# A state-space scan loop in units of two states, with softplus summed by TensorE

## The reference, cut to what matters

```python
dt = jax.nn.softplus(dt @ dt_w.T + dt_b)
A = -jnp.exp(A_log)
dA = jnp.exp(dt[..., None] * A)
dBx = dt[..., None] * Bm[:, :, None, :] * xc[..., None]
def step(h, inp):
    dA_t, dBx_t, C_t = inp
    h = dA_t * h + dBx_t
    y = jnp.einsum('bds,bs->bd', h, C_t)
    return (h, y)
y = jnp.swapaxes(ys, 0, 1) + xc * D
y = y * jax.nn.silu(z)
```

## Time and profile before

| what | us |
|---|---|
| median of 3 runs | 899.14 |
| lowest and highest | 898.27, 904.83 |
| the profiled execution | 901.04 |
| span of its trace | 899.3 |

### The profile page before, as it was taken

One profiled execution on the slowest core, in us unless ns is written; L12 is line 12 of the kernel. 1 busy time (PEld: TensorE's weight loads), 2 busy tenths in 40 slices (PEclk: granted clock), 3 DMA queues, 4 the chain that ended last, 5 costly groups with the idle time before them and its releaser, 6 DMA issues. The chain is left out here.

```text
span 899.3 us, 19137 instructions
## 1 busy us (share of the span) xinstructions
PE 708.9 (79%) x7722; PEld 442.3 (49%) x7722; DVE 721.3 (80%) x938; ACT 369.3 (41%) x585; POOL 516.2 (57%) x407
## 2 busy tenths in 40 slices
PE   7987886699877387788878878887887787787696
PEld 3554553356554154544544544454454454446363
DVE  3998887763320489999999989999999999974998
ACT  2220002156536755545555555555455554321000
POOL 5000000000010489999999999999999999970043
PEclk9999998889989799999999999999999999998799
DMA  4000000000004256666666665666667666600001
GB/s 162 5 4 4 5 4 2 3 1 1 1 1 126 74 171 210 197 187 190 212 194 188 197 203 177 189 209 196 189 189 213 187 198 205 195 30 1 0 12 41
DMA packets 55866, 102.81 MB, mean 114 GB/s; under 512 B 11169, under 2 KB 13345, under 8 KB 55777
## 3 DMA queue, kind: packets, MB, share of 16 engines
q1 hardware_dynamic: 55552, 100.73, 36.6%
q0 software_dynamic: 224, 0.85, 0.2%
HBM read 98.00 MB, written 3.54 MB: 113 GB/s over the span
## 5 line engine op out<-in xcount | busy, mean ns | idle before, releaser
L546 POOL TENSOR_TENSOR ring<-ring,big 128x576 f32<-128x576 f32 x206 | 285.1, 1406 | 13.7 <-DVE ring L936 11.8
L184 PE MATMUL banks<-ring,main_params 128*128 128x288 f32 x824 | 244.2, 426 | 4.6 <-POOL ring L546 2.8
L936 DVE TENSOR_TENSOR_SCAN ring<-big,banks 128x576 f32<-128x576 f32 x154 | 202.6, 1340 | 2.3
L184 PEld LDWEIGHTS banks<-ring,main_params 128*128 128x128 f32 x824 | 146.4, 192 | 60.0 <-POOL ring L546 15.7
L924 DVE TENSOR_TENSOR banks<-banks,big 128x576 f32<-128x576 f32 x192 | 143.0, 745 | 24.0 <-PE banks L1218 21.4
L718 ACT ACTIVATE big<-big,small 128x576 f32<-128x576 f32 x192 | 142.2, 764 | 27.3 <-DVE ring L936 21.5
L523 POOL COPY big<-normed 128x288 f32<-128x288 f32 x8 | 3.0, 429 | 244.2 <-DVE normed L422 244.2
L1217 PE MATMUL banks<-big,selectors 96*128 96x512 bf16 x192 | 74.5, 390 | 80.0 <-DVE ring L936 37.4
L356 PE MATMUL banks<-big 32*32 32x288 f32 x3712 | 96.9, 429 | 21.3 <-issue 17.2
L790 DVE SCALAR_TENSOR_TENSOR big<-big 128x288 f32<-128x288 f32 x216 | 93.6, 512 | 0.0
L718 ACT ACTIVATE banks<-big,small 128x576 f32<-128x576 f32 x64 | 47.4, 741 | 108.2 <-DVE ring L936 86.9
(11 more groups left out here) (166 smaller groups left out, 962.5 us busy)
## 6 DMA issues: line engine op xcount, KB each, us to landing
big<-bc_rows SPq DMA_DIRECT2D x640, 144.0 KB, 3.2
bc_rows<-big SPq DMA_DIRECT2D x16, 144.0 KB, 2.4
residual<-x_in SPq DMA_DIRECT2D x2, 576.0 KB, 5.8
out<-big SPq DMA_DIRECT2D x2, 512.0 KB, 3.0
main_params<-main_in SPq DMA_DIRECT2D x1, 895.0 KB, 8.7
big<-front_in POOLq DMA_DIRECT2D x1, 574.5 KB, 5.7
experts<-experts_in SPq DMA_DIRECT2D x1, 512.0 KB, 9.0
row_selectors<-rows_in POOLq DMA_DIRECT2D x1, 256.0 KB, 5.9
```

The lines of the kernel that those rows point to most:

```text
L184: last = nc.tensor.matmul(PS[rows, 2 * p + a, 0:HALF], lhsT, rhs[:, bass.ds(at + a * HALF, HALF)], start=start, stop=stop, skip_group_chec ...
L546: nc.gpsimd.tensor_tensor(slot, slot, CT[n % 10], ALU.mult).then_inc(weighted, 1)
L936: nc.vector.tensor_tensor_scan(slot, DECAY[m % 3], place, 0.0, ALU.mult, ALU.add).then_inc(scanned, 1)
```

## The change

The loop walks over 128 pairs of states; a tile is now 128x1152, the two states one behind the other.

- `scan` is one instruction over 1152 elements. The decay of step 0 of each state is held at zero (`firsts_zero`, written once by POOL), so that the second state starts afresh; ACT writes steps 1 to 575 of each (`decay`, still one instruction per state, always to SBUF).
- `spread_b` writes both rows to PSUM banks 0 to 3, the only place for them. `inputs_on_dve` reads them there and writes the product to the slot in SBUF. The scan then reads decay and input from SBUF and writes the slot.
- `inputs_on_pool` (pairs 3 and 7 of an image) and `weigh` are 1152 wide. `DTX` is read twice through a broadcast axis.
- The sum of softplus leaves POOL: `add_sizes` (PE, four matmuls with the identity into banks 4 and 5) and `sizes` (ACT, a copy to `DT`). All side work uses banks 4 and 5 and stands at pairs of its own.
- Buffers in states: C 8 (was 10), B 4 (was 3), decay 6 (was 3), slots 14 (was 10; two of the seven pairs in `XN`), `STAGE` 2 (was 3). SP issues half as many loads, each twice as long.

```diff
-        POOL_U = (3, 7, 11, 15)
-        V_AFTER, BC_AFTER = 1, 9
-        AHEAD = 2
+        SPARE_PAIR = 2
+        POOL_U = (3, 7)
+        POOL_AHEAD = (3, 2)
+        SIZES_AT = 3
...
             def step_sizes(b):
-                pool.wait_ge(sp_set, b + 1)
-                nc.gpsimd.tensor_tensor(DT[b % 3], DT[b % 3], TMP[b % 2], ALU.add).then_inc(dt_set, 1)
                 pool.wait_ge(dt_set, b + 1)
...
-                nc.gpsimd.tensor_tensor(SLOT[n % SLOTS], BT[m % 3], DTX[n // DS % 2], ALU.mult).then_inc(u_pool, 1)
+                nc.gpsimd.tensor_tensor(both(SLOT[k % SLOTS]), both(BT[m % 2]), twice(DTX[k // HS % 2]), ALU.mult).then_inc(u_pool, 1)
...
-                nc.gpsimd.tensor_tensor(slot, slot, CT[n % 10], ALU.mult).then_inc(weighted, 1)
+                nc.gpsimd.tensor_tensor(SLOT[k % SLOTS], SLOT[k % SLOTS], CT[k % 4], ALU.mult).then_inc(weighted, 1)
...
+            def sizes(b):
+
+                act.wait_ge(dt_mm, b + 1)
+                nc.scalar.activation(img(DT[b % 3], 0), pair(SPARE_PAIR), ACT.Copy).then_inc(dt_set, 1)
...
-                u = row(place_of(("tile", n)))
-                nc.vector.tensor_tensor(u, u, DTX[n // DS % 2], ALU.mult).then_inc(u_dve, 1)
+            def inputs_on_dve(k):
+                dve.wait_ge(b_spread, DVE_PAIRS.index(k) + 1)
+                dve.wait_ge(dtx_set, k // HS + 1)
+                wait_slot(dve, k)
+                nc.vector.tensor_tensor(both(SLOT[k % SLOTS]), rows_pair(), twice(DTX[k // HS % 2]), ALU.mult).then_inc(u_dve, 1)
...
-                    nc.vector.tensor_tensor_scan(slot, place, slot, 0.0, ALU.mult, ALU.add).then_inc(scanned, 1)
...
-                    nc.vector.tensor_tensor_scan(slot, DECAY[m % 3], place, 0.0, ALU.mult, ALU.add).then_inc(scanned, 1)
+                slot = SLOT[k % SLOTS]
+                nc.vector.tensor_tensor_scan(slot, DECAY[k % 3], slot, 0.0, ALU.mult, ALU.add).then_inc(scanned, 1)
...
+            def add_sizes(b):
+
+                pe.wait_ge(sp_set, b + 1)
+                pair_matmul(SPARE_PAIR, par("ident"), DT[b % 3], 0, stop=False)
+                pair_matmul(SPARE_PAIR, par("ident"), TMP[b % 2], 0, start=False).then_inc(dt_mm, 1)
```

More of the change, by code:

```diff
@@ L29 @@
 DR = 2
-NTILES = B * DS
+HS = DS // 2
+NPAIRS = B * HS
 BR = 3 * 2 * DS
@@ L147, in build_program @@
         SQ = RING[:, 0:N]
-        SLOT = [RING[:, i * L:(i + 1) * L] for i in range(8)] + MORE
+        SLOT = ([RING[:, 2 * i * L:2 * (i + 1) * L] for i in range(4)] + [MORE] +
+                [XN[:, 2 * i * L:2 * (i + 1) * L] for i in range(2)])
         SLOTS = len(SLOT)
@@ L263, in gelus, with both, twice, wait_slot @@
             return 2 * l + a if l < 2 else 4 + GROUPS * a
[L265 to L290, removed]
+        POOL_PAIRS = [k for k in range(NPAIRS) if k % HS in POOL_U]
+        DVE_PAIRS = [k for k in range(NPAIRS) if k % HS not in POOL_U]
+        def both(t):
+            return t.rearrange("p (y t) -> p y t", y=2)
+        def twice(t):
+            return t.unsqueeze(1).to_broadcast([128, 2, L])
+        def wait_slot(engine, k):
+            if k >= SLOTS:
+                engine.wait_ge(y_added, 2 * (k - SLOTS + 1))
         def image(t, i):
@@ new lines, in weigh @@
+            def weigh(k):
+                pool.wait_ge(scanned, k + 1)
+                pool.wait_ge(c_loaded[k % 4], 32 * (k // 4 + 1))
+                nc.gpsimd.tensor_tensor(SLOT[k % SLOTS], SLOT[k % SLOTS], CT[k % 4], ALU.mult).then_inc(weighted, 1)
+            step_sizes(0)
+            for k in range(NPAIRS + 1):
+                if k >= 1:
+                    weigh(k - 1)
+                for at, ahead in zip(POOL_U, POOL_AHEAD):
+                    if k < NPAIRS and k % HS == at - ahead:
+                        inputs_on_pool(k + ahead)
+                if k < NPAIRS and k % HS == SIZES_AT and k // HS + 1 < B:
+                    step_sizes(k // HS + 1)
@@ L720, in _ @@
-            act.wait_ge(a_set, 1)
[L721 to L735, removed]
+                if k >= 3:
+                    act.wait_ge(scanned, k - 2)
@@ new lines, in decay @@
+                nc.scalar.activation(both(DECAY[k % 3])[:, y, 1:L], DT[b % 3][:, 1:L], ACT.Exp, scale=ANEG[:, s:s + 1]).then_inc(decay_set, 1)
+            act.wait_ge(a_set, 1)
+            for k in range(-2, NPAIRS):
+                j, b = k % HS, k // HS + PREPARED
+                if k + 2 < NPAIRS:
+                    for y in range(2):
+                        decay(k + 2, y)
+                if j == 7 and k // HS + 2 < B:
+                    for step in (0, 1):
+                        softplus(k // HS + 2, step)
+                if k < 0:
+                    continue
+                if j == 0 and k // HS + 1 < B:
+                    for step in (2, 3):
+                        softplus(k // HS + 1, step)
+                if j == 2 and k // HS + 1 < B:
+                    sizes(k // HS + 1)
+                if b < B and j == 3:
+                    step_inputs(b, SPARE_PAIR)
+                if b < B and j == 4:
+                    stage_rows(b, SPARE_PAIR)
+                if b < B and j == 5:
+                    middle(b, SPARE_PAIR)
+                if b < B and j == 6:
+                    low(b, SPARE_PAIR)
```

219 lines of the change are left out of this document (104 added, 115 removed).

## The result

The changed kernel takes 1134.3 us (median of 4 runs, 1131.9 to 1134.9), the kernel before 898.7 on the same chip (4 runs, 896.8 to 904.8). The ratio is 1.260, with a 95% interval of 1.254 to 1.266. The prediction said 1162, from 1095 to 1210. The direction and the mechanism hold; the pace is 28 us better than forecast over the whole kernel, and why is the main question left. The profiled execution took 1134.7 us against 901.0 before.

A forecast was written before the change was run, and what follows sets the result against it. POOL set the pace before, DVE one microsecond behind; after, their exclusion would. The loop: 5.9 + 16 x 47.5 - 1.4 + 2.1 = 766.6 us against 503.5, +263 on 901.0 gives 1164, or 1162 against the median; range 1095 to 1210.

The forecast's parts named there:

- Where the scan's operands lie: DVE scans with both operands in SBUF and POOL instructions exclude each other, in whole instructions; chance 0.84.
- rival without contention: The scan's second operand has DVE's own path; DVE sets the pace at 28.9 an image, 872 us (865 to 885); chance 0.09.
- the one with sharing: Scan and POOL take turns element by element: 37.3 us an image, 1007 us (960 to 1060); chance 0.07.
- `L918` as the first witness: Before the loop, this 128x16 DVE instruction took 1.37 us, ending 0.03 after POOL's: POOL can hold DVE.
- third row: DVE needs a second path for two SBUF operands; `L443`, with only one, ran in 1.01 us beside POOL.
- The sum under exclusion: Per image, 8 scans at 2.54 and POOL's 10 x 2.62 + 1.41 cannot overlap; 47.5 us after hand-overs, bounds 44.7 to 51.5.
- Start, 5.9 us: From softplus to first scan: four matmuls 2.27, copy 0.75, `DTX` 1.41, first input 1.35, hops 0.1; 4.4 before.
- Behind the last weigh, 2.1: At the loop's end: four matmuls 1.22 and the gate 0.75, with hops 2.1 us.
- PE, 12.8 us of 47.5: PE's 42 fp32 matmuls an image, at 1.22 us for four, fit beside the exclusion and cost nothing.
- Inputs at 1.35, unchanged, beside POOL: Sign in the changed profile: DVE's wide input (line 936) keeps its 1.35 us length while POOL works.
- A clock that may fall: PE's clock may fall, as in the first window (0.78); at 1.2 GHz its matmuls take 23.8 us and still fit.
- DVE's own 28.9 an image: DVE's work per image without contention: 8 scans x 2.45, 6 inputs x 1.44 and 0.66 for the gate.

The follow-up runs named there:

- the pair by itself: Separate kernel computing nothing of the reference: six DVE and six POOL instructions side by side; six scans take 26.64 us beside POOL's multiply, 14.77 with one operand in PSUM.
- the place alone: Kernel before, with the product of 12 DVE states an image written to the SBUF slot and scanned there: 1089.1 us, 1.205 of before.
- the kernel with less for PE: Changed kernel with the sum of softplus back on POOL, off PE and ACT: 1151.9 us, 1.275 of before.

## Why the prediction was right, and where it was off

- *"Where the scan's operands lie", exclusion:* right, and shown three ways: the pair by itself (26.64 against 14.77), the place alone (+188 us), and a `weigh` that reads nothing (no loss). The rival without contention and the one with sharing fall. By sharing a scan would add some 1.2 us to a POOL instruction (1152 fetches at 1.05 ns); it adds 4.85 - 2.57 = 2.28, near its whole streaming time of 2.40, and the ends are in step.
- *`L918` as the first witness:* here the forecast had luck. The hold was read rightly, but `L918` is a `tensor_scalar` with one SBUF tensor to read, which by the forecast's own third row (`L443`) could do without the shared path. The kernel of pairs shows its kind to be a case apart: beside it six memsets took 9.10 instead of 6.06, while beside two-operand scans they took 6.05. So `L918` showed that POOL can hold DVE, and not that it holds a scan with two SBUF operands; from the rows alone that stayed open, as the first rival says.
- *The sum under exclusion, 47.5 an image:* measured 45.22. The mis-sized term is the durations of its first line. It took whole instructions, 2.54 and 2.62, took 0.13 off for each take-over by DVE and put 0.07 on for each by POOL. Only streaming holds: 8 x 2.40 + 10 x 2.43 + 1.22 = 44.7, which stood in the text as the lower bound; 0.5 of 45.2 is what remains at the turns without a scan, where POOL's pitch of 2.6 has its fixed part. 16 x 2.3 = 37 us too much. `L918`, on which the 0.13 rested, is too short to show that POOL's fixed part too lies beside the scan.
- *Start, 5.9 us:* it took 314.50 - 306.42 = 8.1. The term of four matmuls was mis-sized: a sum of four fp32 matmuls has eight records, 4.18 us on a PE that had idled, and not 2.27. *Behind the last weigh, 2.1:* 3.0 (from 1035.99 to 1039.03), with the same error in it.
- *PE, 12.8 us of 47.5:* 31.5 of 45. The row that gave 1.22 for four matmuls holds two, for the same reason, so 42 of them would be 25.6 at the full clock; and the spread rows were left out. The conclusion held: DVE waits for POOL's inputs in this loop, once an image, not for PE.
- *Inputs at 1.35, unchanged, beside POOL:* 1.33. *A clock that may fall:* 0.82, at no cost that shows: DVE's inputs wait 0.1 us for PE's rows, and the kernel with less for PE is slower.
- The errors nearly close the sum: 8.1 + 16 x 45.22 - 1.4 + 3.0 = 733.2, against 732.6 measured. The 4.4 us of a later start have no cause in the change that could be found; the trace has one new gap there, at 287 us in the convolutions, where PE stood idle for 3.06 us with no wait that the profile shows.
- *DVE's own 28.9 an image* was a number of the rival, and right: the kernel whose POOL only writes runs at 30.88 with 2.0 of stretched scans in it, and DVE busy for 30.25 of it.

## What to carry to other kernels

Before moving an intermediate from PSUM to SBUF, look at which engine reads it together with what: in these runs a DVE scan or multiply with two SBUF operands stood still while GpSimd streamed from SBUF, and the other way round, and the sum of both streaming times became the pace. Where GpSimd is the bound of a loop, keep one DVE operand in PSUM. Look for the loss in the mean durations by form, not in the idle times; and halving the count of an operation saves only its fixed part, which the longer wait for its input can eat.

## What the runs showed of the hardware

- The exclusion has no price beyond itself. Scan and multiply alternate strictly, at 4.85 us a pair for 2.40 + 2.43 of streaming. The Trainium skill ("SBUF — State Buffer", section "SBUF: two separate sides") says that the first to come has the shared pair for the whole instruction. The trace agrees but for the ends: by the sum of the pair, the fixed parts (0.14 and 0.19, worked out from rows) lie beside the other's work. What its section "Who interferes with whom" says of a GpSimd instruction that only writes agrees: memsets of 6.05 for six beside two-operand scans of 14.80.
- It is different beside DVE's `tensor_scalar` from SBUF to SBUF, with one tensor to read. Six of POOL's multiplies then took 18.01 instead of 15.44, and six memsets 9.10 instead of 6.06:
```profile
271.54 9.10 POOL L108 MEMSET gout<- 128x1152 f32 x6 [0.68 <-DVE vout L103]
```
- A broadcast second operand costs POOL nothing: 15.44 for six multiplies with it and without.
- An fp32 matmul leaves two records: `add_sizes` issues four matmuls, and its row of the timeline says x8.
- The granted clock was 0.82 in a window of the loop where PE was busy 31.5 of 45 us, and 1.00 in one where it was busy 25.1 of 31.
